# A selective scan on one core: the conv taps folded into the projection, batch 1 prepared in batch 0's loop

## The reference, cut to what matters

```python
h = rmsnorm(layernorm(x))          # L0a; in L3a the second norm is a layer norm with weight and bias
u, z = split(h @ in_proj)          # 256 channels each
u = silu(causal_conv4(u) + conv_b) # 4 taps per channel, along the positions
dt, B, C = split(u @ x_proj)       # rank 8 (L0a) or 1 (L3a), 16, 16
dt = softplus(dt @ dt_proj + dt_b)
s = s * exp(dt * A_n) + dt * u * B_n   # scan over positions, for each of 16 states n
y = (sum_n s * C_n + u * D) * silu(z)
out = y @ out_proj                 # L0a goes on with a residual, an rms norm and a three-layer MLP
```

## Time and profile before

| | us |
|---|---|
| Median of 3 runs (lowest to highest) | 3445.13 (3442.0 to 3448.75) |
| The profiled execution, its own time | 3442.52 |
| Its span, from first to last instruction | 3440.9 |
| Mean granted clock of TensorE | 0.893 |

### The profile page before, as it was taken

One profiled execution on the slowest core, in us unless ns is written; L12 is line 12 of the kernel. 1 busy time (PEld: TensorE's weight loads), 2 busy tenths in 40 slices (PEclk: granted clock), 3 DMA queues, 4 the chain that ended last, 5 costly groups with the idle time before them and its releaser, 6 DMA issues. The chain is left out here.

```text
span 3440.9 us, 33444 instructions
## 1 busy us (share of the span) xinstructions
PE 2647.8 (77%) x11658; PEld 1159.7 (34%) x11666; DVE 1726.3 (50%) x2715; ACT 1450.1 (42%) x2368; POOL 576.3 (17%) x564
## 2 busy tenths in 40 slices
PE   3567778999879789466745677889997897985677
PEld 1221264444334233123212212735443442431232
DVE  3867541555131721695648675425552227127955
ACT  2443502655234444443425445036552344444444
POOL 0432000000002411260006220000000024113500
PEclk8898968999979899799878989599999898997998
DMA  2002000000010210000000020000000102100000
GB/s 100 0 0 63 12 1 0 1 1 1 0 49 0 75 50 0 0 0 1 1 13 0 1 66 9 1 0 1 1 1 1 49 4 72 49 0 0 0 2 7
DMA packets 36752, 54.59 MB, mean 16 GB/s; under 512 B 7648, under 2 KB 19936, under 8 KB 36576
## 3 DMA queue, kind: packets, MB, share of 16 engines
q1 hardware_dynamic: 32224, 48.42, 4.3%
q10 hardware_dynamic: 4352, 3.94, 0.4%
HBM read 38.44 MB, written 13.63 MB: 15 GB/s over the span
## 5 line engine op out<-in xcount | busy, mean ns | idle before, releaser
L1709 ACT ACTIVATE L1b_pr<-ps,L1b_mneg 128x512 f32<-128x512 f32 x256 | 173.7, 683 | 195.7 <-DVE L1b_mneg L1748 195.7
L518 POOL TENSOR_TENSOR xs<-xs,L2f_part 128x512 f32<-128x512 f32 x32 | 40.5, 1265 | 1286.7 <-DVE L2f_part L507 1286.7
L90 ACT ACT_TABLE_LOAD x34 | 43.6, 1283 | 412.1 <-PEq L671 180.5
L1746 DVE TENSOR_REDUCE L1b_m<-ps 128x2 f32<-128x1024 f32 x128 | 156.8, 1225 | 105.0 <-PE ps L1613 101.0
L1046 POOL TENSOR_TENSOR L3a_db<-L3a_du,L3a_bs 128x1024 f32<-128x1024 f32 x64 | 150.4, 2354 | 225.2 <-ACT L3a_bs L1017 214.7
L1046 POOL TENSOR_TENSOR L0a_db<-L0a_du,L0a_bs 128x1024 f32<-128x1024 f32 x64 | 150.4, 2354 | 224.0 <-ACT L0a_bs L1017 213.5
L1416 ACT ACTIVATE L0b_pt<-ps 128x1024 f32<-128x1024 f32 x128 | 129.3, 1024 | 117.6 <-PE ps L1316 115.5
L1504 DVE TENSOR_REDUCE L0b_mx<-ps 128x1 f32<-128x512 f32 x256 | 159.0, 683 | 36.7 <-PE ps L1303 35.2
L1772 DVE COPY L1b_prt<-ps 128x512 f32<-128x512 f32 x128 | 88.5, 692 | 124.9 <-PE ps L1624 124.6
L1122 DVE TENSOR_TENSOR_SCAN L0a_hs<-ps,L0a_db 128x1024 f32<-128x1024 f32 x64 | 146.1, 2282 | 9.6 <-ACT ps L1009 8.0
L1122 DVE TENSOR_TENSOR_SCAN L3a_hs<-ps,L3a_db 128x1024 f32<-128x1024 f32 x64 | 146.1, 2283 | 9.4 <-ACT ps L1009 8.0
(11 more groups left out here) (556 smaller groups left out, 5471.1 us busy)
## 6 DMA issues: line engine op xcount, KB each, us to landing
L2f_w<-expert_dram SPq DMA_DIRECT2D x32, 256.0 KB, 3.0
L2g_w<-expert_dram SPq DMA_DIRECT2D x32, 256.0 KB, 3.0
weights<-w_dram SPq DMA_DIRECT2D x7, 852.5 KB, 9.3
L0b_qs<-stack_dram SPq DMA_DIRECT2D x32, 96.0 KB, 2.2
stack_dram<-L0b_cut SPq DMA_DIRECT2D x24, 128.0 KB, 2.2
L2b_qs<-stack_dram SPq DMA_DIRECT2D x32, 96.0 KB, 2.2
stack_dram<-L2b_cut SPq DMA_DIRECT2D x24, 128.0 KB, 2.1
L0b_ks<-stack_dram SPq DMA_DIRECT2D x28, 96.0 KB, 2.3
```

The lines of the kernel that those rows point to most:

```text
L1709: act.activation(pr[:, s % 2, h, :], g.ps[:, 2 * (s % 2) + h, :], ACT.Exp, bias=mneg[:, s % 2, h:h + 1], accum_out=total[:, u % 2, t, h:h ...
L1746: dve.tensor_reduce(m[:, s % 2, :], g.ps[:, 2 * (s % 2):2 * (s % 2) + 2, :], AX.X, ALU.max).then_inc(max_raw, 1)
```

## The change

- In `prepare`, GpSimd multiplies the projection's u half by each of the four taps. The constants get `_taps`, 1,024 columns for each of the two layers, in place of `_cw`, 8 columns. The convolution becomes four matmuls for each half, summed in PSUM, over a normed input `xin` with three zero columns ahead.
- The second norm is worked out from the first's variance: var / (var + eps) + eps, then Ln and Exp. L3a's second mean and centring are gone.
- Batch 1's x projection, dt, cut rows and du are issued around or in the loop: `take_x(1)` ahead of it, `dt_magnitude(1)` at step 1 and `dt_soft(1)` at step 3 on ScalarE, `dt_positive(1)` at step 0 and `dt_add(1)` at step 5 on VectorE, `split_rows(1)` after input 6 and du after input 10 on GpSimd. Batch 0's y is made after step 17.
- Tiles of the loop have three buffers. A product with C can be given to GpSimd by `on_pool(n)`.
- Two loads of the combined table set stand in `dt_soft`. In L0a's tail each batch goes on by itself where it can.

```diff
+            def _(pool):                       # prepare, on GpSimd
+                pool.wait_ge(loaded, 16 * cut)
+                for name in ("m0", "m3"):
+                    rows = g.w(name + "_taps").rearrange("p (j e) -> p j e", j=4)
+                    pool.tensor_tensor(rows, rows, bcast(g.w(name + "_in", 0, 2 * P), 1, 4), ALU.mult).then_inc(taps, 1)
...
+    def on_pool(n):
+        return 99 <= n < steps - 1 and n % 3 == 2
...
+                def convolve(b, f):            # TensorE
...
+                    for j in range(4):
+                        mm = pe.matmul(g.ps[:, CONV[b] + f, :], g.w(w + "_taps", j * 2 * P + f * P, P), xin[:, b, j:j + T], start=(j == 0), stop=(j == 3))
...
+                def add_state(n):
+                    b, s = n // NS, n % NS
+                    wait_weighed(pe, n)
+                    if n == 0:
+                        pe.wait_ge(dt_abs, 2 * NB)
+                    if s == 0 and b >= 1:
+                        pe.wait_ge(y_steps, b)
...
+                convolve(0, 0)
+                convolve(0, 1)
+                project_z(0)
+                project_x(0)
+                project_dt(0)
+                convolve(1, 0)
+                pe.wait_ge(conv_half, 3)
                 spread_b(0)
+                convolve(1, 1)
+                project_z(1)
+                pe.wait_ge(conv_half, 4)
+                spread_c(0)
                 spread_b(1)
+                project_x(1)
+                project_dt(1)
                 for n in range(steps):
                     if n + 2 < steps:
                         spread_b(n + 2)
                     if n + 1 < steps:
                         spread_c(n + 1)
+                    add_state(n)
...
+                    act.activation(y[:, b, 1, :], ln.sq[:, b, :], ACT.Exp, scale=-1.0).then_inc(inv_var, 1)
+                    act.activation(y[:, b, 0, :], ln.sq[:, b, :], ACT.Exp, scale=-0.5).then_inc(ln.rstd, 1)
+                for b in range(NB):
+                    act.wait_ge(again, b + 1)
+                    act.activation(y[:, b, 1, :], y[:, b, 1, :], ACT.Ln, bias=g.w(eps)).then_inc(again_log, 1)
+                    act.wait_ge(again_log, b + 1)
+                    act.activation(y[:, b, 1, :], y[:, b, 1, :], ACT.Exp, scale=-0.5).then_inc(again_r, 1)
...
+                def dt_soft(b):
                     act.wait_ge(dt_exp, b + 1)
+                    load_exp_ln(g.nc)
                     act.activation(du[:, b, :, :], du[:, b, :, :], ACT.Ln, bias=1.0).then_inc(dt_log, 1)
...
+                tanh_u(0, 0)                   # ScalarE
+                tanh_u(0, 1)
+                tanh_z(0)
+                take_x(0)
+                dt_magnitude(0)
+                dt_soft(0)
+                take_b(0)
                 act.wait_ge(cleared, 1)
                 decays(0)
+                tanh_u(1, 0)
+                tanh_u(1, 1)
+                tanh_z(1)
                 take_b(1)
+                take_x(1)
                 for n in range(steps):
                     if n + 1 < steps:
                         decays(n + 1)
+                    if n == 1:
+                        dt_magnitude(1)
                     if n + 2 < steps:
                         take_b(n + 2)
+                    if n == 3:
+                        dt_soft(1)
...
+                for n in range(steps):         # GpSimd
+                    make_input(n)
+                    if n == 6:
+                        split_rows(1)
+                    if n == 10:
+                        pool.wait_ge(dt_sum, NB)
+                        pool.wait_ge(u_ready, 2 * NB)
+                        pool.tensor_tensor(du[:, 1, :, :], dt[:, 1, :, :], u[:, 1, :, :], ALU.mult).then_inc(dt_ready1, 1)
...
+                    dve.wait_ge(inv_var, b + 1)    # VectorE
+                    dve.tensor_tensor(y[:, b, 1, :], y[:, b, 1, :], g.ps[:, ln.vb[b], :], ALU.mult).then_inc(again, 1)
...
+                halve(0, 0)
+                make_u(0, 0)
+                halve(0, 1)
+                make_u(0, 1)
+                make_gate(0)
+                dt_positive(0)
+                split_rows(0)
+                halve(1, 0)
+                dt_add(0)
+                dve.wait_ge(gate_ready, 1)
+                dve.memset(g.ps[:, DECAY:DECAY + 4, 0:1], 0.0).then_inc(cleared, 1)
+                dve.wait_ge(dt_sum, 1)
+                dve.wait_ge(u_ready, 2)
+                dve.tensor_tensor(du[:, 0, :, :], dt[:, 0, :, :], u[:, 0, :, :], ALU.mult).then_inc(dt_ready, 1)
+                halve(1, 1)
+                make_u(1, 0)
+                make_u(1, 1)
+                make_gate(1)
...
                 for n in range(steps):
...
+                    if n == 0:
+                        dt_positive(1)
+                    if n == 5:
+                        dt_add(1)
+                    if n == NS + 1:
+                        finish(0)
+                finish(NB - 1)
```

More of the change, by code:

```diff
@@ L827, in mamba, with by_pool, by_dve @@
     KP = 96 + (8 if variant == 0 else 1)
+    eps, scale_of = (("eps6", "m0_rms1"), ("eps5", "m3_nw"))[variant]
+    steps = NB * NS
+    B_ROW, C_ROW, SUM, DECAY = 0, 1, 2, 4
+    CONV, GATE, XP, DT = (4, 0), (6, 2), (4, 2), ((5, 4), (3, 2))
+    def on_pool(n):
+        return 99 <= n < steps - 1 and n % 3 == 2
+    def by_pool(n):
+        return sum(on_pool(i) for i in range(n + 1))
+    def by_dve(n):
+        return n + 1 - by_pool(n)
     st = Stage(g, name)
@@ L856, in mamba @@
-        cleared = st.sem("cleared")
-        steps = NB * NS
-        B_ROW, C_ROW, DECAY = 2, 3, 4
+        inv_var, again, again_log, again_r, x_mid, x_in, pads = (
+            st.sem(n) for n in ("inv_var", "again", "again_log", "again_r", "x_mid", "x_in", "pads"))
+        conv, conv_half, conv_tanh, u_ready, z, z_tanh, gate_ready = (
+            st.sem(n) for n in ("conv", "conv_half", "conv_tanh", "u_ready", "z", "z_tanh", "gate_ready"))
+        xp, xp_in, cut_step, split, dtp, dt_pos, dt_abs, dt_exp, dt_log, dt_sum, dt_ready, dt_ready1 = (
+            st.sem(n) for n in ("xp", "xp_in", "cut_step", "split", "dtp", "dt_pos", "dt_abs", "dt_exp", "dt_log", "dt_sum", "dt_ready", "dt_ready1"))
@@ L863, in decay_banks, with wait_weighed @@
             return g.ps[:, at:at + 2, :]
[L865 to L878 removed]
+        def wait_weighed(engine, n):
+            if on_pool(n):
+                engine.wait_ge(weighed_pool, by_pool(n))
+            else:
+                engine.wait_ge(weighed, by_dve(n))
         with g.nc.Block() as block:
@@ new lines, in project_z, with project_x @@
+                def project_z(b):
+                    if b == 1:
+                        pe.wait_ge(again, NB)
+                    for f in range(2):
+                        mm = pe.matmul(g.ps[:, GATE[b] + f, :], g.w(w + "_in", (2 + f) * P, P), xin[:, b, 3:3 + T], start=True, stop=True)
+                    mm.then_inc(z, 1)
+                def project_x(b):
+                    pe.wait_ge(u_ready, 2 * b + 2)
+                    if b == 1:
+                        pe.wait_ge(gate_ready, 2)
@@ L969, in _ @@
                         for k in range(2):
[L970 removed]
+                            mm = pe.matmul(g.ps[:, 6 + b, :], g.w("m0_fc3", k * P, P), du[:, b, k, :], start=(k == 0), stop=(k == 1))
                         mm.then_inc(mlp_h, 1)
@@ L995, in _, with tanh_z, take_x, dt_magnitude @@
+                def tanh_z(b):
+                    act.wait_ge(z, b + 1)
+                    act.activation(gate[:, b, :, :], g.ps[:, GATE[b]:GATE[b] + 2, :], ACT.Tanh, scale=0.5).then_inc(z_tanh, 1)
+                def take_x(b):
+                    act.wait_ge(xp, b + 1)
+                    act.activation(dbc[:, b, :], g.ps[0:KP, XP[b], :], ACT.Copy).then_inc(xp_in, 1)
+                def dt_magnitude(b):
                     for k in range(2):
-                        act.activation(du[:, b, k, :], g.ps[:, 6 + k, :], ACT.Abs, bias=g.w(w + "_dtb", k, 1)).then_inc(dt_abs, 1)
+                        act.wait_ge(dt_pos, 2 * b + k + 1)
+                        act.activation(du[:, b, k, :], g.ps[:, DT[b][k], :], ACT.Abs, bias=g.w(w + "_dtb", k, 1)).then_inc(dt_abs, 1)
@@ new lines, in _ @@
+                for n in range(steps):
[6 more added lines that the diff above has]
+                        pool.tensor_tensor(du[:, 1, :, :], dt[:, 1, :, :], u[:, 1, :, :], ALU.mult).then_inc(dt_ready1, 1)
+                    if n >= 2 and on_pool(n - 2):
+                        weigh(n - 2)
+                for n in range(steps - 2, steps):
+                    if on_pool(n):
+                        weigh(n)
@@ L2232, in mamba @@
         put(p + "_in", in_w)
-        put(p + "_cw", np.asarray(conv_w).reshape(2, 128, 4).transpose(1, 0, 2).reshape(128, 8))
+        put(p + "_taps", over(np.asarray(conv_w).T.reshape(-1)))
         put(p + "_cb", col(conv_b))
```

345 lines of the change are left out of this document (164 added, 181 removed).

## The result

| | before | after |
|---|---|---|
| Median (lowest to highest), four runs each | 3446.94 (3442.0 to 3452.36) | 3335.34 (3331.42 to 3343.99) |
| Ratio of the two, 95% interval | | 0.968 (0.9655 to 0.9704) |
| The profiled execution, its span | 3442.5, 3440.9 | 3331.42, 3329.9 |
| Mean granted clock | 0.893 | 0.903 |

The change gains 111.0 us of span; 158 were forecast and 3314 was the upper end of the range, so more gain was forecast than came. A second profile of the same changed kernel later gave a median of 3334.31 (five runs).

What follows compares the result with a forecast made beforehand. It took VectorE to bound the loops and a chain that no engine fills to bound the openings. 148.2 - 7 + 19.6 - 2.8 = 158 us saved from 3442.5 gave 3285 us, range 3264 to 3314.

Steps and rivals of the forecast that it cites:

- Part 1: Openings, from a layer's first matmul to its first scan: 304.2 us fall to 156.0 over four runs, 148.2 saved.
- Part 2: Loop: the added work and stalls lengthen each run from 116.6 to 118.3 us, 1.7 lost per run, 7 in all.
- 1.2 of stall: Loop start: TensorE's sum of step 0 waits for batch 1's Abs with B row 3 behind it; scan 3 1.2 us late.
- split_rows ... call it 0.7: Loop: GpSimd's cutting of batch 1's rows takes 4.2 us, mostly covered; 0.7 lost per run, bounds 0 and 3.
- covered by the same 2.5: Loop: batch 1's du (2.35 us, behind input 10) fits the 2.5 us that GpSimd can be late, costing nothing.
- Rival 1: Loop: late items in three in-order queues lie bare, 38 us more, 3322 in all, or half of it, 3304; chance 0.14.
- Rival 2: VectorE's dt_add and u blocked by GpSimd: in full 19 us more, 3304, chance 0.04; mild 3290, within the forecast's 0.66.
- Part 3: L0a's tail: table loads go and fc2 starts earlier, 9.8 us saved, twice: 19.6.
- Rival 3: L0a's tail: Ln and Exp still load tables, so only some 3 of the 9.8 us are saved, 3299; chance 0.10.
- Part 4: Loading, once: 1.02 MB more costs 2.8 us; blocking between GpSimd and VectorE could add up to 4.7, not counted.
- Rival 5: Openings and loop: less is added than counted, without stalls in start or split, 3270; within the forecast's 0.66.
- Rival 4: TensorE's clock stays low in openings and loop: 3457, slower, chance 0.01; in the opening alone 3353, chance 0.05.

Runs made afterwards that it cites:

- the fill: Changed kernel with TensorE spreading the C row of step 1 thirteen times instead of once, keeping it busy before the sum of step 0: 3328.42 us.
- the early release: Changed kernel with batch 1's two Abs on ScalarE moved from step 1 to step 0, one decay earlier: 3314.19 us.
- the earlier release: Changed kernel with batch 0's y made after step 16 instead of step 17: 3330.51 us.
- the spread cutting: Changed kernel with GpSimd's five cutting instructions placed one behind each of inputs 6 to 10, and du behind input 12: 3323.88 us.
- the run with the table alone: Kernel before, with the combined Exp and Ln table set loaded ahead of dt's Ln: 3446.35 us beside 3450.86, ratio 0.9987.

## Why the prediction was wrong

**Part 1 held.** The openings save 146.2, against 148.2. The order of the walk was right to the releaser; the error is 0.3 us ahead of the first convolution and 0.7 behind it, in L0a's first run.

**Part 2 failed: "1.7 lost per run, 7 in all".** It was 10.6 per run, 42.4 in all. Three of its steps are at fault: the price of TensorE's late sums, the price of the cutting beside dt_add, and a wait at scan 1 that it put at nothing.

- "1.2 of stall" at scan 3 was 3.2, and "0.6 is new" at scan 19 was 2.9. The text said of TensorE that "its work per step fits only at 2.4 GHz" and then priced both stalls at the high clock, although its own rows have the sum of step 0 at 3.62. In the kernel before, the sums of steps 0 and 16 took 3.07 to 3.62 and 3.21 to 3.62 over the four runs, and scans 3 and 19 lost at most 0.8. So the slow sum was there already and nearly free; the change releases it late. The time of release was forecast right (batch 1's Abs end 36.8 after the first convolution), the sum's length was not. An estimate from the rows of the changed kernel and of the fill: with the sum at 1.88, B row 3 would be copied 2.1 earlier and 1.1 of stall be left, close to the 1.2. With the early release and the sum as slow as ever, 1.0 to 1.4 are left. So late and slow together make the 3.2; late alone is an estimate, since the fill held up other work. At scans 18 to 22 the earlier release alone brought 2.4.
- "split_rows ... call it 0.7": it holds GpSimd for 5.3 us, inside the bounds given (up to 6.7), and dt_add and the cuts block each other. The two together cost 3.8 instead of 1.9. Another 1.3 are lost at scans 10 to 14, around du behind input 10, which was costed at nothing since "covered by the same 2.5". That the cutting had used up this cover four steps before is the likely reason, but no run moves du alone. With the cutting spread and du two steps later, nothing is lost at scans 7, 10 and 11.
- dt_positive(1) was costed at its 1.41. It also waits for dt of batch 1, for which TensorE must run project_x(1) behind gate(1): 0.66 more at the high clock, 2.3 and above at the low. The wait that the change adds had no term.

More sums run slow than before: those of step 6 or 7 and of step 19 in all four runs (3.17 to 3.62), none of them in the kernel before. What these alone cost no run shows.

**Rival 1** is what happened, "three in-order queues ... gain a late item each". Its price, 38 us more where all of it lies bare and 3322 for the whole, was close for the loops (35 more than forecast) and had a chance of 0.14. That closeness is partly luck: it adds up GpSimd's and ScalarE's work, while of the 8.7 a run by which the losses above exceed the forecast, 1.1 at scan 1 and 2.3 at scan 19 come from TensorE's work, which is in none of its terms.

**Rival 2** was right in mechanism and small in the change: dt_add took 1.32 to 1.61, and u(1,0) 0.94 beside the end of GpSimd's first product, where u(1,1) took 0.68. It stood at its full price in the spread cutting, 3.75. The Trainium skill, SBUF — State Buffer, section "Who interferes with whom", says that a VectorE instruction with two SBUF inputs contends with a GpSimd one that reads SBUF and that the order of issue decides who blocks. These rows agree: dt_add beside the product (3.75 against 1.22), y's second instruction beside it (1.72 against 1.22), and GpSimd's cast behind dt_add (1.49 against 0.60). On the order of issue they are not all plain: in the spread cutting dt_add's record begins 0.32 ahead of the product's, inside a cast of GpSimd's, and the product still runs its normal 2.34 while dt_add waits.

**Part 3 held**: 19.9 against 19.6, of which the run with the table alone gives 11.2 to the tables. Rival 3 is out.

**Part 4 held in its first term and failed in the choice of 2.8.** 2.3 are the transfer. The text bounded the blocking by 4.7 and took 0; it was 2.9. (Its 1.02 MB should read 1.04: 2,032 columns of 512 bytes.)

**Elsewhere**: nothing was forecast, and 7.5 were lost in the profile. The second profile of the kernel before shows L2b longer by 5.1 in its two runs and L1b by 6.6, with unchanged code. All unchanged layers together took 2549.5 and 2559.5 in the two profiles of the kernel before, and 2557.1 and 2556.7 in those of the changed kernel. So these 7.5 can't be laid on the change. L2b alone took 121.3 to 121.8 in its four runs after and 116.5 to 121.6 before, but also 118.4 in the run with nothing of batch 1 in the loop and 122.1 in the kernel before with the table edit.

**The sum**: 146.2 + 19.9 - 42.4 - 5.2 - 7.5 = 111.0. **Rival 5** is out, since more was added to the loops than counted. **Rival 4** did not decide: the openings' clock was 0.91, and the loop's 0.92 in mean. But the mean of a stretch was the wrong row to lean on. It hid that slow records sit where TensorE's work has been released late, and there others wait for them. A wait alone does not tell the level: in the middle of the loop TensorE waits 1.13 us in every step and its sums take 1.88.

## What to carry to other kernels

Work moved into a loop costs more than its own time: for each piece list what stands behind its wait on its own engine, and price TensorE's work behind a new wait at both levels of the clock, since the rows of before can show which records are slow already. Pieces of one step each, spread over several, fit where one lump does not; that a slack once spent stays spent for some steps is likely here, but not shown alone. Keep VectorE instructions with two SBUF inputs out of the time in which GpSimd works, or between a scan and its product, and put the copy that feeds the next step ahead of any wait that isn't needed for it. Release the late item earlier first: that brought the most here, with the clock as low as before.

## What the runs showed of the hardware

- In one kernel, one piece of TensorE's work falls to either level from run to run: project_x(1) of the changed kernel, behind 2.03 us of waiting each time, took 1.93 us in three runs and 3.62 in the fourth; over the kernels scan 1 lost 2.1 or 3.7 to 5.1 with it and with the dt matmuls behind it (1.98 or 3.8).
- A sum behind 1.02 and 1.12 us of idle ran at the low clock (3.65), one behind the fill at the high one (1.88), and in the steady loop the sums stay at the high one although TensorE waits 1.13 us in each step.
- VectorE's tensor_scalar of 128x128, with one such input and a column of thresholds, took 1.12 and 2.38 us beside GpSimd's product in the loading, and 0.29 and 0.28 without it: blocking is not confined to instructions with two full inputs.
- Layers with no changed code moved by up to 6.6 us between two profiles of one kernel. A part's gain of a few us is read from that part's rows, not from the total.
